# The second expert layer computed over sorted tokens in two parts

## The chip, the cores and the metric

The kernel runs on one core of a Trainium2 chip. The metric is the device time in microseconds (us) of one execution; lower is better. TensorE (PE) multiplies, VectorE (DVE), ScalarE (ACT) and GpSimd (POOL) do the rest, and SyncE (SP) issues the plain DMAs. TensorE's clock has two levels, 1.2 and 2.4 GHz; the profile shows the granted clock as a share of 2.4.

## The reference, cut to what matters

The input x holds 8 batches of 256 tokens of 128 channels, 2048 tokens, that is 16 token tiles of 128. Eight layers are added to it in turn: cross attention (att0), a mixing layer (ffn0), attention (att1), experts (moe1), attention (att2), experts (moe2), attention (att3), experts (moe3). The change rewrites moe2, whose reference is:

```python
def _L2_ffn_ref(x, ln_g, ln_b, rW, rb, W1, b1, W2, b2):
    z = _layernorm(x, ln_g, ln_b)              # E = 8 experts, TOP_K = 2
    probs = jax.nn.softmax(jnp.einsum('bth,he->bte', z, rW) + rb, axis=-1)
    topv, topi = jax.lax.top_k(probs, TOP_K)
    mask = jnp.sum(jax.nn.one_hot(topi, E, dtype=probs.dtype) * topv[..., None], axis=-2)
    w = mask / jnp.maximum(jnp.sum(mask, axis=-1, keepdims=True), 1e-08)
    hid = jax.nn.gelu(jnp.einsum('bth,ehf->btef', z, W1) + b1, approximate=False)
    outs = jnp.einsum('btef,efh->bteh', hid, W2) + b2
    return x + jnp.sum(outs * w[..., None], axis=2)
x = x + _L2_ffn_ref(_layernorm(x, axis=-1), ...)
```

Each token's result needs two of the eight experts only. W1 is 128x256 and W2 256x128 for each expert, all in float32.

## The kernel before, in words

The program is written out by hand, engine by engine, with semaphores. Each engine goes through the stages in the same order, and within a stage through numbered steps; where work of the next stage is put among the steps of this one, tables say so.

**Attention stages (att0, att1, att2).** They are pipelines over batches. A step of att2 has 8 beats u, one for each head; batch b is projected in one step, its row maxima are taken in the next, its columns, exponentials and averages follow, and it is finished and added to x (`residual`, L865) in the fourth. `steps_of` (L461) numbers the steps by `tail`, so that tail 0 is the first step in which no new batch starts, and (tail, u) names a place. The row maxima are DVE's (L912), eight in a step; PE may run at most two heads ahead of them. After the last batch there are four tail steps, 0 to 3.

**moe1, sorted.** The tokens are sorted by expert in two parts of 8 token tiles. For each part the router's logits are taken, a chain of small DVE operations picks two experts for a token (`route_pick`, L1101), `mark_picks` (L1139) marks them, PE ranks them (`rank_tokens`, L2241), and `place_tokens` (L1150) works out a row in a list of 23 tiles of 128 rows for each pick, each tile having one expert, and each tile's expert. POOL then scatters each token tile twice to DRAM by an indirect DMA (`send_row`, L1508 to L1523), 16 of them in a part; each waits for the third before it (IN_FLIGHT = 3). SP loads the lists' tiles back, two at a time, up to six ahead (`load_tile`, L660), when all sends of the part have landed. 46 tiles then go through a software pipeline (`sorted_tiles` on each engine; on PE L2265 to L2302). In its iteration j PE transposes tile j+2 (L2275), multiplies tile j+1 by the up and gate weights (L2280, 512 columns), transposes the hidden tile j (L2288) and multiplies tile j-1 by the down weights (L2295). ACT copies the transposed tile (L1810), takes the activation (L1815) and copies the transposed hidden tile (L1819); DVE multiplies the gate (L1247) and copies the output (L1254); SP stores it (L690). POOL fetches each token's two rows by indirect DMAs (`fetch_output`, L1525 to L1541), and DVE adds them to x by their weights (`join_outputs`, L1189). For the second part all routing pieces stand in iterations -2 to 3 (SORT_BEATS), its sends among tiles 4 to 17, and the joins of the first half in iterations 30 to 42; the second half is joined within att2's batches.

**moe2, dense.** All 8 experts are computed for all tokens, in 4 blocks of 512 tokens (`block_of` on PE, ACT and DVE; the middle two blocks are a hardware loop). For each expert and block PE does two up products of 512 columns (L2312), ACT a Gelu with bias on each (L1831), PE eight down products of 128 columns (L2224), and DVE four weighted additions to x (`add_y`, L1294). Its first 12 token tiles are normalised in tail steps 1 and 2 of att2: moments (L822, L829), the power -1/2 on POOL (`make_rstd_all`, L1389), the normalised tiles z (L837), transposed in tail step 2 (L1890). The last 4 follow after the last batch. Routing and the terms for bias and residual stand beside the first block (`beside_first_block`), and the first 12 tiles of att3 are normalised beside the last.

**att3** has one head. Its ten steps (`single_head`, from L2151 on PE) need att3's normalised tiles, 2 for each step, and x itself only for the addition at the end of a batch, two steps later: POOL adds the bias to x (`add_bias`, L1413), DVE adds the projection (L1060).

The names in the tables of the change: stats, rstd, norm, turn and turned are normalisation and transposing; logits, top, exp, first, second, mark, rank, place, weigh and load are the routing pieces in their order. Lines are those of the kernel before.

## Time and profile before

| | us |
|---|---|
| median of 3 runs | 861.91 (858.91 to 865.30) |
| the profiled execution's own time | 864.2 |
| its span, first to last instruction | 862.3 |
| PE busy in the span | 717.4 (83%) |
| DVE busy | 483.3 (56%) |
| ACT busy | 394.5 (46%) |
| POOL busy | 238.6 (28%) |
| mean granted TensorE clock | 0.938 |

The profiled execution took 2.3 us more than the median. In the rows below times are from the start of the span. In a timeline row the first number is the start, the second the time from the first start to the last end of the instructions merged in it, then engine, line, operation, output<-input, partitions x elements and type, the count, and in brackets the idle time before it with what ended it. The profile counts a float32 product as two matmul instructions and a float32 transpose as one.

### The profile page before, as it was taken

What the parts mean: (1) busy time and instruction counts of PE and PEld (TensorE: products, weight loads), DVE (VectorE), ACT (ScalarE), POOL (GpSimd) and SP (SyncE); (2) the same over time, 40 slices, a digit from 0 to 9 for tenths busy, and PEclk for the clock granted to TensorE, in tenths of its full rate; (3) what the DMA queues carried; (4) which work ended last, traced back from release to release, by engine and by line L of the source; (5) the groups of instructions that cost most, each with busy time, mean ns of one, the idle gap of its engine ahead of it and who ended that gap; (6) DMA issues with size and microseconds to landing.
All of it is one profiled execution on the core that took longest, in us unless ns stands there. A gap on an engine that the chain in (4) does not pass through costs nothing. (4 is left out here: it accounts for less than half of the span.)

```text
span 862.3 us, 14733 instructions
## 1 busy us (share of the span) xinstructions
PE 717.4 (83%) x4784; PEld 486.7 (56%) x4784; DVE 483.3 (56%) x1392; ACT 394.5 (46%) x837; POOL 238.6 (28%) x382
## 2 busy tenths in 40 slices
PE   1487788899998777998868786899999786679998
PEld 1255565556665445565534554667777675446665
DVE  4458756776777633435566865673335334444443
ACT  2356464466765454454425555453343454222221
POOL 3344454333331261516366543100001002000000
PEclk9999999999999895999958999799999999689999
DMA  9623323332222001333272320000000200033331
GB/s 272 168 57 99 93 52 92 89 94 69 64 58 58 11 34 32 102 90 107 81 205 67 82 75 2 1 1 1 1 0 1 83 1 0 3 88 97 98 97 63
DMA packets 76320, 57.96 MB, mean 67 GB/s; under 512 B 7400, under 2 KB 70120, under 8 KB 75768
## 3 DMA queue, kind: packets, MB, share of 16 engines
q1 hardware_dynamic: 74200, 52.85, 22.3%
q0 software_dynamic: 2048, 4.20, 1.6%
q8 instruction: 39, 0.64, 0.3%
q14 instruction: 33, 0.27, 0.1%
HBM read 25.37 MB, written 9.24 MB: 40 GB/s over the span
## 5 line engine op out<-in xcount | busy, mean ns | idle before, releaser
L912 DVE TENSOR_REDUCE negmax<-ps 128x2 f32<-128x512 f32 x256 | 169.5, 685 | 107.0 <-PE ps L1965 106.0
L1658 ACT ACTIVATE exps<-ps 128x512 f32<-128x512 f32 x256 | 148.3, 598 | 101.0 <-PE ps L1977 96.5
L1965 PE MATMUL ps<-stack 96*128 96x256 bf16 x512 | 103.6, 297 | 36.5 <-DVE negmax L912 20.0
L1977 PE MATMUL ps<-stack 99*128 99x256 bf16 x512 | 99.8, 285 | 18.5 <-DMA stack<-maxt 14.0
L1965 PEld LDWEIGHTS ps<-stack 96*128 96x128 bf16 x512 | 47.9, 103 | 62.0 <-DVE negmax L912 35.6
L1977 PEld LDWEIGHTS ps<-stack 99*128 99x128 bf16 x512 | 43.6, 100 | 60.1 <-DMA stack<-maxt 22.7
L1993 PE MATMUL ps<-exps,values 128*32 128x256 f32 x1024 | 73.3, 403 | 1.4 <-ACT exps L1658 1.4
L2224 PEld LDWEIGHTS ps<-pack_moe,ht 128*128 128x128 f32 x512 | 62.7, 194 | 16.4 <-issue 14.6
L1294 DVE SCALAR_TENSOR_TENSOR x_sb<-ps,weights,x_sb 128x128 f32<-128x128 f32 (+1 forms) x128 | 36.0, 344 | 61.8 <-PE ps L2224 61.6
L1831 ACT ACTIVATE ht<-ps,pack_moe 128x512 f32<-128x512 f32 x64 | 43.3, 686 | 57.6 <-PE ps L2312 56.0
L2224 PE MATMUL ps<-pack_moe,ht 128*128 128x128 f32 x512 | 63.0, 277 | 0.5 <-ACT ht L1831 0.5
L2312 PE MATMUL ps<-zt,pack_moe 128*128 128x512 f32 (+1 forms) x128 | 62.5, 611 | 0.0
L1844 ACT ACTIVATE gated<-ps 128x512 f32<-128x512 f32 x36 | 21.5, 597 | 76.4 <-PE ps L2341 76.4
L2280 PE MATMUL ps<-pack_moe,gated 128*128 x92 | 50.3, 630 | 0.0
L2352 PEld LDWEIGHTS ps<-pack_moe,ht 128*128 128x128 f32 x288 | 37.6, 193 | 19.8 <-issue 13.5
L1381 POOL TENSOR_SCALAR var_eps<-moments 128x12 f32<-128x12 f32 (+4 forms) x9 | 1.8, 201 | 166.3 <-DVE moments L829 136.1
L1284 DVE TENSOR_TENSOR ht<-ps,gated 128x512 f32<-128x512 f32 x36 | 24.9, 691 | 39.1 <-ACT gated L1844 39.0
L1523 POOL DMA_INDIRECT gathered<-z,placed x32 | 31.3, 980 | 52.6 <-DVE placed L1177 30.8
L1993 PEld LDWEIGHTS ps<-exps,values 128*32 128x32 f32 x1024 | 29.9, 113 | 21.3 <-issue 7.4
L2352 PE MATMUL ps<-pack_moe,ht 128*128 128x128 f32 x288 | 38.6, 277 | 2.7 <-DVE ht L1284 2.7
L1541 POOL DMA_INDIRECT late<-outputs_moe,placed x32 | 31.5, 986 | 31.1 <-DMA outputs_moe<-y_kept 15.7
L1468 POOL TENSOR_TENSOR qk_rest<-qk,qk_parts 128x512 f32<-128x512 f32 x24 | 27.8, 1157 | 44.3 <-DVE qk_parts L923 44.2
(221 smaller groups left out, 1317.0 us busy)
## 6 DMA issues: line engine op xcount, KB each, us to landing
stack<-qk_parts SPq DMA_DIRECT2D x168, 128.0 KB
stack<-weights_t SPq DMA_DIRECT2D x32, 256.0 KB, 3.2
pack_moe<-in_moe SPq DMA_DIRECT2D x1, 3076.0 KB, 16.4
outputs_moe<-y_kept SPq DMA_DIRECT2D x46, 64.0 KB
ht<-gathered SPq DMA_DIRECT2D x22, 128.0 KB
gathered<-y_kept SPq DMA_DIRECT2D x10, 256.0 KB, 3.6
pack_moe<-in_moe SPq DMA_DIRECT2D x1, 2129.0 KB
pack_moe<-in_moe SPq DMA_DIRECT2D x1, 1732.0 KB, 6.9
```

The source lines that it names most:

```text
L912: dve.tensor_reduce(negmax_of[b % 2][:, :, h:h + 1].rearrange("p t h -> p (t h)"), ps[:, h % 2, :].rearrange("p (t k) -> p t k", t=2), AX, ...
L1294: last = dve.scalar_tensor_tensor(out=xt, in0=ps[:, 4 + e % 2, t * D:(t + 1) * D], scalar=w, in1=xt, op0=ALU.mult, op1=ALU.add)
L1541: pool.indirect_dma_start(back[:, n, :], None, averaged[s, g], at).then_inc(back_in[n], 16)
L1658: nc.scalar.activation(exps[:, i, :], ps[:, 2 + h % 2, :], ACT.Exp, scale=scale)\
L1831: nc.scalar.activation(ht[:, e % 2, c, :], ps[:, 2 * (e % 2) + c, :], ACT.Gelu, bias=par(s, "b1")[:, k:k + 1]).then_inc(sem["h_ready"], 1)
L1965: last = pe.matmul(ps[:, h % 2, t * T:(t + 1) * T], st[0:MAXROW, h, 0, t * P:(t + 1) * P], st[0:MAXROW, h, 1, :], start=True, stop=True)
L1977: last = pe.matmul(ps[:, 2 + h % 2, t * T:(t + 1) * T], st[0:MAXROW + 3, h, 1, t * P:(t + 1) * P], st[0:MAXROW + 3, h, 0, :], start=True, ...
L1993: last = pe.matmul(ps[STRIP * k:STRIP * (k + 1), AV, r * T:(r + 1) * T], values[nh][:, buf(s, a), kt, u, :], exps[:, slot(s, a, u), kt * T ...
L2224: last = pe.matmul(ps[:, 4 + e % 2, t * D:(t + 1) * D], ht[:, e % 2, c, t * P:(t + 1) * P], par(s, "w2")[:, k * P:(k + 1) * P], start=(c = ...
L2280: pe.matmul(ps[:, (j + 1) % 2, :], taken_t[:, (j + 1) % 2, :], par(s, "experts")[:, bass.ds(at, 2 * T)], start=True, stop=True).then_inc(s ...
L2312: pe.matmul(ps[:, 2 * (e % 2) + c, :], par(s, "w1")[:, k * P:(k + 1) * P], zt[:, bass.ds(2 * blk, 2), 1:1 + T], start=True, stop=True).the ...
L2352: last = pe.matmul(ps[:, 4 + blk % 2, t * D:(t + 1) * D], ht[:, q % 2, 0, t * P:(t + 1) * P], par(s, "w2")[:, w * P:(w + 1) * P], start=(q ...
```

## The change

moe2 becomes sorted like moe1, with these differences. The up product has 256 columns in place of 512, there is no gate, and a bias is added within PSUM by a product of 3 rows of ones with 3 bfloat16 rows of biases (b1 and b2, each split in three parts). ACT's work for a tile is one copy with scale and bias and one Gelu; the copy of the transposed hidden tile is DVE's. The lists, tiles and weights are of the same size and number: 46 tiles, 23 in each part.

For the first part (token tiles 0 to 7) the normalisation and all routing pieces are put into att2's steps from tail -2 to tail 2, and its 16 sends at one per beat from tail 1, beat 1. Tiles 8 to 13 are normalised in tail 2 and 3, tiles 14 and 15 after the last batch. The second part's routing pieces are put one by one into iterations -1 to 8 of the tiles, its sends after tiles 9 to 22. The kept part of x (x plus its normalised value) is worked out by one DVE operation on a token tile in each of the iterations 5 to 20. The outputs of token tiles 0 to 7 are fetched and joined in iterations 25 to 43; those of tiles 8 to 15 at the start of att3: 16 fetches on POOL with the first additions of biases among them, and joins at the ends of DVE's steps 0 to 3. att3's normalisation goes in four groups of 4 token tiles: the first at tiles 36 to 41, the second right after the tiles, the third and the fourth in steps 1 to 5. The biases are split on POOL at the start of moe1 and spread by three small DMAs at the start of att2. The dense code of moe2 goes. moe1 and moe3 compute as before.

```diff
-    "moe2": [("router", 8), ("rb", 8), ("xg", 1), ("xb", 1), ("w1", 2048), ("b1", 16), ("w2", 2048), ("b2", 128)],
+    "moe2": [("router", 8), ("rb", 8), ("xg", 1), ("xb", 1), ("experts", 4096)],
...
-SORTED = ("moe1",)
-EXPERT = {"moe1": 768}
+SORTED = ("moe1", "moe2")
+EXPERT = {"moe1": 768, "moe2": 512}
...
+NORMED = {"moe1": (range(0, 8), range(8, 14), range(14, NT)), "moe2": (range(0, 6), range(6, 8), range(8, 14), range(14, NT))}
...
+    "moe2": {"stats": ((-2, 5), (-1, 5), (2, 5)), "rstd": ((-2, 7), (-1, 7), (2, 5)), "norm": ((-1, 0), (0, 0), (3, 5)),
+             "turn": ((-1, 2), (-1, 4), (0, 1), (3, 5), (3, 6)), "turned": ((-1, 3), (-1, 5), (0, 2), (3, 6), (3, 7)),
+             "logits": (0, 2), "top": (0, 3), "exp": (0, 4), "first": (0, 5), "second": (0, 6), "mark": (0, 7), "rank": (1, 0),
+             "place": (1, 1), "weigh": (1, 3), "load": (2, 3), "logits2": (3, 7)}}
+SEND_FROM = {"moe1": 14, "moe2": 9}
+SEND_EVERY = {"moe1": 2, "moe2": 1}
...
+              "moe2": {"logits": -1, "top": 0, "exp": 0, "first": 2, "second": 4, "mark": 5, "rank": 5, "weigh": 6,
+                       "place": 7, "load": 8}}
...
+JOIN_TILES = {"moe1": (30, 32, 33, 34, 36, 38, 40, 42), "moe2": (29, 31, 33, 35, 37, 39, 41, 43)}
+PLUS_TILES = range(5, 5 + NT)
+JOIN_STEPS = {0: (8,), 1: (9, 10, 11), 2: (12,), 3: (13, 14, 15)}
+LAST_TILES = {"stats": 36, "norm": 39, "turn": 40}
...
+SEND_TILE = {"moe1": 4, "moe2": 9}
...
+GROUPS = {"moe1": PART, "moe2": PART, "att3": tuple(range(t, t + BT) for t in range(0, NT, BT)),
...
-            sp.wait_ge(sem["x_updated"], done("x_updated", "moe2", 99))
+            pass_tiles("moe2")
+            wait(sp, "y_psum", "moe2", 0)
...
+                        sp.wait_ge(bias_split, 5)
+                        for k in range(3):
+                            sp.dma_start(bias_rows[k:k + 1, :], split[:, k, :]).then_inc(bias_in, 16)
...
+            def keep_of_norm(s):
+                r1 = rstd[:, 1, :]
+                dve.tensor_scalar(keep[:, 0, :], r1, 1.0, None, ALU.add).then_inc(sem["x_plus"], 1)
+                dve.scalar_tensor_tensor(out=keep[:, 1, :], in0=moments[:, :, 0], scalar=-1.0, in1=r1, op0=ALU.mult, op1=ALU.mult)\
+                    .then_inc(sem["x_plus"], 1)
+                wait(dve, "x_plus", s, 0, 1)
+            def plus_norm(s, t):
+                dve.tensor_scalar(x_sb[:, t, :], x_sb[:, t, :], keep[:, 0, t:t + 1], keep[:, 1, t:t + 1], ALU.mult, ALU.add)\
+                    .then_inc(sem["x_plus"], 1)
...
+                    if step in (2, 4):
+                        apply_all(s, step // 2 + 1, GROUPS[s][step // 2 + 1])
...
+                    if step in JOIN_STEPS:
+                        for t in JOIN_STEPS[step]:
+                            join_outputs("moe2", t)
+                    if step in (1, 3):
+                        stats_all(s, step // 2 + 2, GROUPS[s][step // 2 + 2])
...
+                if s == "moe2" and j == PLUS_TILES[0]:
+                    keep_of_norm(s)
+                if s == "moe2" and j in PLUS_TILES:
+                    plus_norm(s, PLUS_TILES.index(j))
+                if j in JOIN_TILES[s]:
+                    join_outputs(s, JOIN_TILES[s].index(j))
+                if s == "moe2":
+                    if j == LAST_TILES["stats"]:
+                        dve.wait_ge(loaded["att3"], 16)
+                        stats_all("att3", 0, GROUPS["att3"][0])
+                    if j == LAST_TILES["norm"]:
+                        apply_all("att3", 0, GROUPS["att3"][0])
...
+                    if s == "moe2" and 0 <= j < ALL_TILES:
+                        dve.wait_ge(sem["ht_psum"], done("ht_psum", s, 0, j))
+                        dve.wait_ge(sem["y_psum"], done("y_psum", s, 0, j - 2)) if j >= 2 else None
+                        dve.tensor_copy(turned[:, j % 2, :], ps[:, 3, 0:T]).then_inc(sem["ht_ready"], 1)
...
-            def add_y(s, blk, e):
-                wait(dve, "y_psum", s, blk, e)
-                wait(dve, "x_updated", s, blk, e - 1)
-                for t in range(BT):
-                    xt = x_sb[:, bass.ds(blk * BT + t, 1), :].rearrange("p a d -> p (a d)")
-                    w = weights[:, bass.ds(blk * BT + t, 1), e:e + 1].rearrange("p a d -> p (a d)")
-                    last = dve.scalar_tensor_tensor(out=xt, in0=ps[:, 4 + e % 2, t * D:(t + 1) * D],
-                                                    scalar=w, in1=xt, op0=ALU.mult, op1=ALU.add)
-                last.then_inc(sem["x_updated"], 1)
...
-                    wait(pool, "taken_psum", s, 0, SEND_TILE + n * 9 // 10)
+                    wait(pool, "taken_psum", s, 0, SEND_TILE[s] + n * 9 // 10)
...
+                    if s == "moe2" and t == 6:
+                        pool.wait_ge(loaded["att3"], 16)
+                        make_rstd_all("att3", 0, GROUPS["att3"][0])
...
+                    for t in range(2 * FETCHED_EARLY, NT):
+                        for k in range(2):
+                            fetch_output("moe2", t, k)
+                        if t == 11:
+                            add_bias(s, 0)
+                        if t == 13:
+                            make_rstd_all(s, 2, GROUPS[s][2])
+                            add_bias(s, 1)
+                    add_bias(s, 2)
+                    make_rstd_all(s, 3, GROUPS[s][3])
...
+            def gelu_tiles(s):
+                for j in range(-2, ALL_TILES):
+                    if 0 <= j + 2 < ALL_TILES:
+                        act.wait_ge(sem["taken_psum"], done("taken_psum", s, 0, j + 2))
+                        act.wait_ge(sem["up_psum"], done("up_psum", s, 0, j)) if j >= 0 else None
+                        nc.scalar.activation(taken_t[:, j % 2, :], ps[:, 2, 0:P], ACT.Identity, bias=par(s, "xb"),
+                                             scale=par(s, "xg")).then_inc(sem["taken_ready"], 1)
+                    if 0 <= j + 1 < ALL_TILES:
+                        i = (j + 1) % 2
+                        act.wait_ge(sem["up_psum"], done("up_psum", s, 0, j + 1))
+                        act.wait_ge(sem["ht_psum"], done("ht_psum", s, 0, j - 1)) if j >= 1 else None
+                        nc.scalar.activation(hidden[:, i, :], ps[:, i, 0:T], ACT.Gelu).then_inc(sem["h_ready"], 1)
+                    if j == SORT_BEATS[s]["exp"]:
+                        route_exp(s, 1)
+                    if j == LAST_TILES["turn"] + 1:
+                        copy_all("att3", [0])
...
+                        w = up_width(s)
+                        last = pe.matmul(ps[:, (j + 1) % 2, 0:w], taken_t[:, (j + 1) % 2, :],
+                                         par(s, "experts")[:, bass.ds(at, w)], start=True, stop=(s == "moe1"))
+                        if s == "moe2":
+                            last = pe.matmul(ps[:, (j + 1) % 2, 0:w], ones16[0:3, :], bias_rows[:, bass.ds(at, w)],
+                                             start=False, stop=True)
...
+                                             par(s, "experts")[:, bass.ds(at + (up_width(s) + c * D), D)], start=(c == 0),
+                                             stop=(c == 1 and s == "moe1"))
+                        if s == "moe2":
+                            last = pe.matmul(ps[:, 4, 0:D], ones16[0:3, :], bias_rows[:, bass.ds(at + up_width(s), D)],
+                                             start=False, stop=True)
...
-                        pe.matmul(ps[:, 2 * (e % 2) + c, :], par(s, "w1")[:, k * P:(k + 1) * P],
-                                  zt[:, bass.ds(2 * blk, 2), 1:1 + T], start=True, stop=True).then_inc(sem["up_psum"], 1)
...
```

## Rows read from the trace of the kernel before

**Rows 1.** Windows, moe2's bulk: stretch, length, busy PE/PEld/DVE/ACT/POOL, clock, DMA share, GB/s.

```profile
576.00:676.00 100.00, 100.00 (x592) 74.06 (x592) 38.48 (x147) 39.52 (x58) 2.48 (x2) 1.00 0.00 1
```

**Rows 2.** Timeline of PE: moe2's first product, and att3's first instruction.

```profile
546.75 1.88 PE L2312 MATMUL ps<-zt,pack_moe 128*128 128x512 f32 x4
...
676.39 0.60 PE L2156 MATMUL ps<-pack_consts,ctx_sb 128*96 128x128 f32 x4
```

**Rows 3.** Timeline of all engines in moe1: PE's work for one tile.

```profile
376.49 0.27 PE L2275 MATMUL ps<-pack_consts,ht 128*128 128x128 f32 x1
...
376.60 1.02 PE L2280 MATMUL ps<-pack_moe,gated 128*128 x2
...
377.46 0.38 PE L2288 MATMUL ps<-pack_consts,ht 128*128 128x128 f32 x2
...
377.68 0.61 PE L2295 MATMUL ps<-pack_moe,ht 128*128 x4
...
378.13 0.27 PE L2275 MATMUL ps<-pack_consts,ht 128*128 128x128 f32 x1
```

**Rows 4.** The same timeline: DVE's work for one tile.

```profile
378.08 0.42 DVE L1247 TENSOR_TENSOR ht<-ps,gated 128x256 f32<-128x256 f32 x1 [1.01 <-ACT gated L1815]
...
378.42 0.28 DVE L1254 COPY y_kept<-ps 128x128 f32<-128x128 f32 x1
```

**Rows 5.** Timeline of POOL: sends of part one and two, powers for 12 tiles.

```profile
324.17 0.96 POOL L1523 DMA_INDIRECT gathered<-z,placed  x1 [0.31 <-issue]
...
366.93 0.96 POOL L1523 DMA_INDIRECT gathered<-z,placed  x1 [0.30 <-issue]
...
728.69 2.28 POOL L1389 TENSOR_TENSOR rstd<-var_eps,neghalf 128x12 f32<-128x12 f32 x1
```

**Rows 6.** Timeline of DVE in att2's tail: after the last maximum, then the normalised tiles.

```profile
523.32 0.24 DVE L858 RECIPROCAL rden<-ps 128x16 f32<-128x16 f32 x1
...
537.41 3.16 DVE L837 TENSOR_SCALAR z<-x_sb,moments,rstd 128x128 f32<-128x128 f32 x12 [4.32 <-POOL rstd L1389]
```

**Rows 7.** Timeline of DVE in moe1: routing pieces, eight operations from the first to the second.

```profile
336.73 0.22 DVE L1109 TENSOR_REDUCE rs<-lg 128x8 f32<-128x64 f32 x1 [0.59 <-ACT lg L1723]
...
338.50 0.23 DVE L1118 SCALAR_TENSOR_TENSOR rt<-rt,lg 128x64 f32<-128x64 f32 x1
```

**Rows 8.** Timeline of SP's queue: the first loads of moe1's tiles.

```profile
326.41 6.94 SPq L672 DMA_DIRECT2D ht<-gathered  x4
```

**Rows 9.** Timeline of PE in moe1: first transposed tile, tile 3's hidden, tile 45's.

```profile
331.53 0.42 PE L2275 MATMUL ps<-pack_consts,ht 128*128 128x128 f32 x1
...
346.27 0.52 PE L2288 MATMUL ps<-pack_consts,ht 128*128 128x128 f32 x2
...
424.27 0.44 PE L2288 MATMUL ps<-pack_consts,ht 128*128 128x128 f32 x2 [0.27 <-DVE ht L1247]
```

**Rows 10.** Windows of moe1's start and its bulk (columns as in rows 1).

```profile
331.50:346.50 15.00, 11.01 (x38) 5.99 (x37) 8.08 (x36) 7.58 (x15) 0.00 (x0) 0.61 0.05 14
346.50:427.00 80.50, 74.98 (x405) 49.64 (x404) 38.23 (x127) 41.59 (x132) 35.93 (x39) 1.00 0.33 94
```

**Rows 11.** Timeline of ACT in moe1: an activation table is loaded.

```profile
335.14 1.28 ACT L1723 ACT_TABLE_LOAD   x1
```

**Rows 12.** Waits in moe1's bulk: engine, line, what it waited for: us, times, longest.

```profile
ACT gated L1810 <- remote: 2.0, 1, 2.0
```

**Rows 13.** The outputs' tensor of moe1: from a fetch's or store's issue to landing.

```profile
DMA to landing us min/median/max: 2.5/2.5/3.1
```

**Rows 14.** Timeline of PE in att3: the projections of two steps in turn.

```profile
701.14 0.70 PE L2165 MATMUL ps<-zt,pack_att 128*128 128x256 f32 x2
...
707.33 0.60 PE L2165 MATMUL ps<-zt,pack_att 128*128 128x256 f32 x2
```

**Rows 15.** Timeline of DVE in att3: the maxima of batch 1, the addition of batch 2.

```profile
688.14 0.69 DVE L1028 TENSOR_REDUCE negmax<-ps 128x2 f32<-128x512 f32 x1 [1.14 <-PE ps L2200]
...
707.53 0.42 DVE L1060 TENSOR_TENSOR x_sb<-ps,xb 128x256 f32<-128x256 f32 x1 [1.91 <-PE ps L1954]
```

More of the change, by code:

```diff
@@ L1410, in add_bias @@
                 wait(pool, "x_updated", s, d - 1)
-                wait(pool, "joined", "moe1", 0, 2 * d + 1) if s == "att2" else None
+                wait(pool, "joined", before(s), 0, 2 * d + 1) if before(s) in SORTED else None
                 bo = par(s, "bo").unsqueeze(1).to_broadcast([P, 2, D])
@@ L1823, in sorted_tiles @@
                         beside_last_tiles(EARLY_TILES.index(j))
-            def block_of(s, blk, first=False, final=False):
-                for e in range(E):
-                    for c in range(2):
-                        k = 2 * e + c
-                        wait(act, "up_psum", s, blk, k)
-                        wait(act, "y_psum", s, blk, e - 2)
-                        nc.scalar.activation(ht[:, e % 2, c, :], ps[:, 2 * (e % 2) + c, :], ACT.Gelu,
-                                             bias=par(s, "b1")[:, k:k + 1]).then_inc(sem["h_ready"], 1)
-                    if first:
-                        beside_first_block(s, e)
-                    if final and s == "moe2" and 5 <= e < 8:
-                        copy_all("att3", range(e - 5, e - 4))
@@ new lines, in experts @@
+            def experts(s):
+                for blk in range(NBLK):
+                    for i in range(E + 1):
+                        wait(act, "up_psum", s, blk, i)
+                        wait(act, "h_ready", s, blk, i - 2) if i >= 2 else wait(act, "h_ready", s, blk - 1)
+                        nc.scalar.activation(gated[:, i % 2, :], ps[:, 2 * (i % 2), :], ACT.Silu)\
+                            .then_inc(sem["gate_done"], 1)
+                        if blk == 0 and i < E:
+                            beside_first_block(s, i)
```

538 lines of the change are left out of this document (225 added, 313 removed), and 1 row of the table PACKS.

## The prediction

> **What bounds the kernel now.** I read the table of 40 slices first, where moe2 is the stretch in which PE is never below 9 tenths. The windows say it sharply: in 100 us of moe2 PE is busy 100.00 us at full clock, DVE 38 and ACT 40 [rows 1]. So PE alone bounds moe2, from its first product at 546.75 to att3's first instruction at 676.39, 129.6 us [rows 2]. Next I read the timeline of moe1, the sorted stage that moe2 is to copy. There the parts of a tile join without a gap: a tile takes 378.13 - 376.49 = 1.64 us, of which the product of 512 columns takes 377.46 - 376.60 = 0.86, two hidden transposes 377.68 - 377.46 = 0.22, two down products 378.13 - 377.68 = 0.45 and the transposed tile 0.11 [rows 3]. DVE needs 0.42 + 0.28 = 0.70 for it [rows 4]. A stage like this has a start, a bulk bound by PE, and a boundary between its parts, and I price moe2 so.
>
> **The change part by part.** It removes the 129.6 us. What comes in their place, from the same point of time on:
>
> *The start, moved later: +14.8.* Before, moe2's products needed only normalised tiles. Now the first tile waits for routing, placing and 16 sends. DVE's last maximum ends about 523.3 [rows 6]. Put among att2's steps before that are the eight tiles' normalisation (3.16/12 = 0.26 for each, 2.1, and as much again for their moments [rows 6]) and the pieces top to mark, some 20 operations at (338.50 - 336.73)/7 = 0.25, 5 us [rows 7]. Some 3 us of these fill gaps, so I count 6: the picks are marked at about 529.5. Ranking by PE and placing (8 operations, 2 us) follow: first send at 533. If the gaps hide all of it, it is 527, if nothing, 536. POOL's queue then holds 16 sends at 0.96 + 0.30 = 1.26, 20.2 us [rows 5]; between them two additions of biases (1.3) and the powers for tiles 8 to 13, as many as the 12 of the row at 2.28, with the two operations before 2.7 [rows 5]. That ends at 557.2, plus 1 for a pause, 558.2; the powers for tiles 14 and 15 stand behind it, 1.4, their tiles 0.7, and the sends' landing with the loads comes to about the same: in moe1 the load was issued 326.41 - 324.17 = 2.2 us after the last send began [rows 5, 8], and I give it 2 more. First transposed tile at 561.5, that is 14.8 after 546.75. Bounds 553 and 566, so +6 to +19. What goes with the old order helps here, and is in these numbers: DVE no longer waits 4.32 us for the powers of 12 tiles before att2's additions [rows 6].
>
> *From the first transposed tile to tile 3's hidden transposes: +10.5.* moe1 took 346.27 - 331.53 = 14.7, at a mean clock of 0.61 [rows 9, 10], since all pieces stood there. moe2 has three table switches between Gelu and the exponential, 3 x 1.28 = 3.8 [rows 11], and two and a half rounds at the lower level of 1.2 GHz, twice 1.4, so 7. Bounds 8 and 15.
>
> *The bulk, 42 tiles: +58.8.* PE's tile is 0.11 + 0.86/2 + 0.22 + 0.45 = 1.21 [rows 3]. The bias products run on 3 rows of bfloat16. No row has that shape; if they cost nothing the tile is 1.21, if as much as the float32 products of 256 and 128 columns, 0.43 + 0.22 more, 1.86. I take a quarter of that, since a float32 product counts as two instructions and each takes longer than a bfloat16 one of the same width: 0.16, and 0.03 for weights that can't load under so short a product; 1.40. DVE's copies (0.70) and the kept part (0.26) lie under it, ACT's copy and Gelu too. The bulk is 42 x 1.40 = 58.8; with the ends, 51 to 78.
>
> *Routing of the second part, tiles 4 to 8: +6.* In these five rounds DVE has 0.70 for the tile and nearly 0.3 for the kept part, with about 32 small operations (second, mark, weigh, place, load) at 0.25 [rows 4, 7]: 5 x 0.96 + 8.1 = 12.9 us against 5 x 1.40 = 7.0 of PE. The rest shows, since DVE goes in order and PE waits for its copy. 3 to 9. Their cover, if any, is the slack between rounds; the piece first, in tile 2, lies under a slow round.
>
> *The boundary at tile 23: +3.5.* The last send waits for the transposing of tile 22. Then: its start to the load's issue 2.2 [rows 5, 8], the load 2.1, releases 0.6; less one round. SP is behind this wait with the stores from tile 17 on, and DVE's copies wait for stores four tiles back; but the stores go out 0.4 us after the load, and land 2.5 later [rows 13], before the copy of tile 21. 0 if POOL is late by nothing and the landing is short, 6 if the sends lag.
>
> *Pauses: +6.5.* moe1's 42 tiles took 424.27 - 346.27 = 78.0 [rows 9] where 42 x 1.64 makes 68.9, and the early pieces of att2 on PE are some 2 of the 9.1. The rest are waits of 1 to 2 us on an engine for which the profile names no releaser but "remote", for instance 2.0 on ACT [rows 12]. moe1's code is written out tile by tile; the dense loop has none of them (100.00 of 100 us [rows 1]). I carry 6.5 over. The Trainium skill, page "Runtime: NRT & Kernel Launch", section on instruction fetch mechanics, says that fetching is hidden in straight code and that taken branches stall, which would favour unrolled tiles over the loop. By that rule this term is 0 and the result 6.5 us lower; the rows on both stages point the other way.
>
> *Joins and att3's tiles, tiles 29 to 45: +2.* Eight joins of two operations fit beside 1.40; the moments in tile 36 and the four normalised tiles in 39 (4 x 0.26) exceed it by some 1.5, the transposes on PE add 0.5. 1 to 4. *Drain: +1.7*, from tile 45's hidden transposes to att3.
>
> Sum: 14.8 + 10.5 + 58.8 + 6 + 3.5 + 6.5 + 2 + 1.7 = 103.8 for 129.6: 25.8 saved.
>
> *att3: +7.* POOL's 16 fetches can begin only when the last output is stored, 2.8 us after att3's first instruction (2.5 landing [rows 13]). At 1.26 each, with additions of biases and powers between, the eighth has landed at 14.7, the twelfth is issued at 18, the last has landed near 28.6. DVE joins tiles 9 to 11 before step 2's maxima: 14.7 + 0.7 + 1.3 of moments, 17 us after the start, where now the maxima of batch 1 come at 688.14 - 676.39 = 11.8 [rows 15]: 5 late. Tiles 13 to 15 hold step 3 in the same way until 30.5; after that the addition of batch 2 comes at 34 against 707.53 - 676.39 = 31.1 [rows 15], 3 late, and the maxima 3 to 5. I add 3 for the landing beside moe3's load, the third transposes and more time at the lower clock. Steps are 707.33 - 701.14 = 6.2 us apart [rows 14], a chain over all engines, so nothing later takes it back. Bounds 3 and 13.
>
> *At nothing:* the split of biases on POOL lies in POOL's wait for moe1's second placing; the three bias DMAs on SP stand at att2's start after the first stacks; moe1 and moe3 keep their work.
>
> Saved 25.8 - 7 = 18.8. Against the profiled execution that is 864.2 - 18.8 = 845.4. The median lies 2.3 below the profiled one, so for it 861.9 - 18.8 = 843.
>
> **The rivals.** A, *the start and att3 hide well*: sends from 527 and landing at once, first tile at 554 (-7.5), att3 only 3 late (-4), bias products at 0.08 (-4): 16 better, 827. For it: POOL is idle in att2's tail and DVE's gap before 537 is 4.3 us [rows 6]. Against: 16 sends have a fixed pitch.
>
> B, *VectorE bounds the round*: copy, copy, kept part, joins and routing in one order, with a releasing delay on each, make the round 1.64 as in moe1, 42 x 0.24 = 10 more, and the late fetches cost att3 10 in place of 7: 856. For it: DVE takes over a copy from ACT. Against: 0.96 of 1.40.
>
> C, the other side: *TensorE's clock stays low.* Waits in the routing rounds and in each tile bring the clock down to 1.2 GHz, and it stays there; each tile then takes 1.40 more. It decides at 18.8/1.4 = 13 tiles; over 30 tiles it is 42, so 885. For it: moe1 began at 0.61 with such gaps. Against: it then ran 80.5 us at 1.00 though PE was idle in 5.5 of them [rows 10]. The Trainium skill, page "TensorE: Matmul & The Clock Gate", section "A second HAM failure mode: psum-queue depth-cycling", tells of a kernel whose clock oscillated from short pauses between groups of matmuls; that speaks for C, and this trace disagrees with it so far.
>
> D, *the sends bound part two*: 16 sends and landings lag, and the boundary becomes 12 us: 852.
>
> **How the numbers follow.** Forecast 0.58, A 0.15, B 0.12, D 0.08, C 0.07. The forecast's own range, from its bounds, is 833 to 854. A and B widen it; with part of C left out I give 826 to 860. A measurement of this kernel tells 1% (8.6 us) from no change. Faster by over 1%, below 853.3: the forecast nearly whole, A, D for the most part: 0.82. Within 1%: most of B, the forecast's edge: 0.11. Slower by over 1%: C: 0.07.
>
> **What would show it.** In PE's timeline: the first transposed tile of moe2 at 561, a round of 1.40 in tiles 10 to 20, one gap near 3.5 us at tile 23, clock 1.00 in the bulk, rounds of 2 to 3 us in tiles 4 to 8 with PE waiting for DVE, att3's first instruction near 650, and DVE waiting for fetches in att3's steps 1 and 3. A round above 1.6, a low clock after tile 10, or a first tile after 566 would make it wrong.

## The result, and the profile after

The changed kernel takes 925.4 us (median of four runs, 911.9 to 935.3), before 863.0 (four runs, 858.9 to 865.3): ratio 1.061, 95% interval 1.051 to 1.071. Forecast were 843 us. The ratio is that of the two faster executions of the changed kernel (911.9 and 918.7, mean clock 0.865 and 0.853; the slower two are 932.1 at 0.833 and 935.3 at 0.830), and the profiled one, with a span of 933.5, is the slowest of the four, so the figures of the trace below are the upper end of the four.

Cut at the same events in both traces: moe1's first transposed tile, moe2's first work (its first transposed tile after the change, its first product before), att3's first context transposes, and the powers for moe3's twelve tiles. Columns are us between them:

| | moe1 begins | to moe2 | moe2 | att3 | rest | span |
|---|---|---|---|---|---|---|
| before | 331.5 | 215.2 | 129.6 | 52.3 | 133.6 | 862.3 |
| after | 327.5 | 243.1 | 157.7 | 68.2 | 137.1 | 933.5 |
| difference | -4.1 | +27.9 | +28.1 | +15.9 | +3.5 | +71.2 |

All three stages that I had priced came out longer. For moe2 the windows of the kernel after (columns as in [rows 1]) answer to [rows 1]:

```profile
580.00:600.00 20.00, 20.00 (x77) 12.70 (x76) 11.24 (x48) 5.05 (x13) 0.78 (x1) 0.50 0.15 41
600.00:620.00 20.00, 20.00 (x69) 12.43 (x67) 7.49 (x25) 5.41 (x13) 7.00 (x8) 0.50 0.21 66
640.00:660.00 20.00, 17.63 (x61) 11.24 (x61) 3.95 (x12) 4.59 (x11) 3.10 (x4) 0.50 0.19 54
700.00:720.00 20.00, 20.00 (x70) 12.99 (x69) 7.16 (x22) 5.72 (x13) 2.03 (x2) 0.50 0.12 34
```

PE is busy all the time, as forecast, but for 2.37 us at the boundary of the parts (in the third line), and the granted clock is 0.50, that is 1.2 of 2.4 GHz, through the whole stage. From 575 to 725 us PE stands still nowhere else, so no work on DVE, ACT or POOL shows any more: at this clock PE hides it all. Its timeline for one tile answers to [rows 3]:

```profile
596.26 0.47 PE L2280 MATMUL ps<-pack_consts,ht 128*128 128x128 f32 x1
596.53 1.06 PE L2286 MATMUL ps<-pack_moe,gated 128*128 x2
597.52 0.39 PE L2289 MATMUL ps<-values,ones 3*128 x1
597.84 0.69 PE L2298 MATMUL ps<-pack_consts,ht 128*128 128x128 f32 x2
598.32 1.06 PE L2305 MATMUL ps<-pack_moe,ht 128*128 x4
599.32 0.28 PE L2309 MATMUL ps<-values,ones 3*128 x1
599.53 0.47 PE L2280 MATMUL ps<-pack_consts,ht 128*128 128x128 f32 x1
```

A tile takes 599.53 - 596.26 = 3.27 us where 1.40 was forecast. The new shape in it is "3*128": the bias products, whose fixed operand has 3 rows. 42 x 3.27 = 137 is nearly the stage.

Ahead of the stage, att2's tail: DVE's last reciprocal, ACT's last copy of averages, and POOL's first and last send of part one, from the timelines of three engines:

```profile
560.23 0.26 DVE L903 RECIPROCAL rden<-ps 128x16 f32<-128x16 f32 x1 [6.49 <-PE ps L2042]
...
558.64 0.38 ACT L1701 ACTIVATE nd<-ps 128x256 f32<-128x256 f32 x1 [8.44 <-remote]
...
540.75 1.10 POOL L1535 DMA_INDIRECT gathered<-z,placed  x1 [4.93 <-PE ps L2002]
...
564.31 0.96 POOL L1535 DMA_INDIRECT gathered<-z,placed  x1 [0.31 <-issue]
```

Counted from moe1's first tile, the last reciprocal is at 232.8 (before: 544.5 - 331.5 = 213.0), so att2 itself became some 20 us longer; the sends begin at 540.75 where I had 533.

### The profile page after: what moved, and what is told of

Read it like the earlier page. It is cut to its first block and busy times, and to the rows that moved or that the text cites. A ratio compares the mean times of both kernels' runs of the same rounds, so it can differ in the third digit from the quotient of the medians.

```text
span 933.5 us, 15053 instructions
## 1 busy us (share of the span) xinstructions
PE 767.9 (82%) x4620; PEld 506.2 (54%) x4620; DVE 493.9 (53%) x1416; ACT 386.3 (41%) x861; POOL 305.3 (33%) x461
## 5 line engine op out<-in xcount | busy, mean ns | idle before, releaser
L1535 POOL DMA_INDIRECT gathered<-z,placed x64 | 62.6, 978 | 117.7 <-DVE placed L1225 60.5
L2286 PE MATMUL ps<-pack_moe,gated 128*128 x184 | 99.6, 635 | 0.0
L1553 POOL DMA_INDIRECT late<-outputs_moe,placed x64 | 62.3, 973 | 80.0 <-DMA outputs_moe<-y_kept 32.0
L2305 PE MATMUL ps<-pack_moe,ht 128*128 x368 | 78.5, 353 | 2.1 <-DVE y_kept L1318 2.0
L1306 DVE COPY ht<-ps 128x256 f32<-128x256 f32 x46 | 19.5, 425 | 69.0 <-PE ps L2298 61.7
L2298 PE MATMUL ps<-pack_consts,ht 128*128 128x128 f32 x184 | 49.9, 365 | 4.6 <-DVE ht L1311 2.5
L1875 ACT ACTIVATE gated<-ps,pack_moe 128x128 f32<-128x128 f32 x46 | 21.0, 457 | 74.1 <-PE ps L2280 70.6
L2298 PEld LDWEIGHTS ps<-pack_consts,ht 128*128 128x128 f32 x184 | 25.9, 173 | 41.7 <-issue 32.5
L1318 DVE COPY y_kept<-ps 128x128 f32<-128x128 f32 x92 | 26.5, 288 | 36.9 <-PE ps L2309 29.2
L2286 PEld LDWEIGHTS ps<-pack_moe,gated 128*128 128x128 f32 x184 | 42.1, 280 | 0.4
```

What stands on the lines that cost most here:

```text
L1535: pool.indirect_dma_start(gathered[g], at, z[:, t, :], None).then_inc(sent[i], 16)
L1553: pool.indirect_dma_start(back[:, n, :], None, averaged[s, g], at).then_inc(back_in[n], 16)
L2286: last = pe.matmul(ps[:, (j + 1) % 2, 0:w], taken_t[:, (j + 1) % 2, :], par(s, "experts")[:, bass.ds(at, w)], start=True, stop=(s == "moe1"))
L2298: last = pe.transpose(ps[:, 3, c * P:(c + 1) * P], hidden[:, j % 2, c * P:(c + 1) * P], ident)
L2305: last = pe.matmul(ps[:, 4, 0:D], turned[:, (j - 1) % 2, c * P:(c + 1) * P], par(s, "experts")[:, bass.ds(at + (up_width(s) + c * D), D)], ...
```

## The experiments

The question was why the clock stays low, then what is left when it doesn't. Kernels with "e2" in their expectation start from e2's code, not from the change; so do those that start from e5 or e7. Where a kernel ran once, its time stands without an interval.

**e1 and e2: take the bias products away, or make them full.** e1's edit:

```
-  start=True, stop=(s == "moe1"))
-  if s == "moe2":
-      last = pe.matmul(ps[:, (j + 1) % 2, 0:w], ones16[0:3, :], bias_rows[:, bass.ds(at, w)], ...)
+  start=True, stop=True)
```

and the same for the down product. e2's:

```
-  bias_rows = values[16]...bitcast(BF16)[0:3, 0:4 * E * P]
+  bias_rows = values[16]...bitcast(BF16)[:, 0:4 * E * P]
+  pool.memset(bias_rows[:, :], 0.0).then_inc(bias_zeroed, 1)      # in moe1, ahead of the three rows' DMAs
-  pe.matmul(..., ones16[0:3, :], bias_rows[:, ...])
+  pe.matmul(..., ones16[:, :], bias_rows[:, ...])
```

> Leaves out moe2's two biases (b1 and b2). Theory A, the bias products, whose fixed operand has 3 rows, are what keeps TensorE's clock at 0.50 in moe2: without them the granted clock is 1.00 there, a tile takes (3.27 - 0.53)/2 = 1.4 us, the stage some 80 us in place of 157.7, and the whole 850 to 862 us. Theory B, the clock is low because of what is left of a tile (a product of 256 columns, two of 128 and three float32 transposes): the clock stays 0.50, a tile takes 3.27 - 0.53 = 2.74 us, the stage some 134 us, the whole 908 to 915 us.

> The same two bias products with a fixed operand of 128 rows in place of 3: the bias rows 3 to 127 are zeros, so the sums are the same and no product is added or taken away. Theory A (the 3 rows are the reason): clock 1.00 in moe2, a tile 1.64 us, the stage 85 to 95 us, the whole 862 to 875 us. Theory B (the rest of the tile): clock 0.50, 3.27 us a tile, the whole within 1% of 925. If e1 is fast and this is slow, the bias products cost the clock for another reason than their rows, for instance by the time they take from the 128-row products.

Measured: e1 870.1 us, ratio to before 1.009 (1.007 to 1.012); e2 877.7, 1.018 (1.013 to 1.023). e2's windows, one of its tiles, and two starts of a tile from e1:

```profile
580.00:600.00 20.00, 15.61 (x112) 11.71 (x111) 14.72 (x62) 8.62 (x20) 5.00 (x5) 1.00 0.25 75
600.00:620.00 20.00, 15.19 (x106) 11.78 (x106) 10.30 (x33) 8.09 (x20) 10.53 (x11) 1.00 0.27 86
```

```profile
629.95 0.28 PE L2283 MATMUL ps<-pack_consts,ht 128*128 128x128 f32 x1
630.07 0.60 PE L2289 MATMUL ps<-pack_moe,gated 128*128 x2
630.51 0.27 PE L2292 MATMUL ps<-values,ones 128*128 x1
630.61 0.38 PE L2301 MATMUL ps<-pack_consts,ht 128*128 128x128 f32 x2
630.83 0.68 PE L2308 MATMUL ps<-pack_moe,ht 128*128 x4
631.34 0.22 PE L2312 MATMUL ps<-values,ones 128*128 x1
631.40 0.28 PE L2283 MATMUL ps<-pack_consts,ht 128*128 128x128 f32 x1
```

```profile
650.03 0.27 PE L2280 MATMUL ps<-pack_consts,ht 128*128 128x128 f32 x1
...
651.31 0.27 PE L2280 MATMUL ps<-pack_consts,ht 128*128 128x128 f32 x1
```

The products are the same in number and width, only their rows differ, and the kernel is 48 us faster by the medians (925.4 - 877.7), 38 us counted from the two faster executions (their mean 915.3); in the two profiled ones the stage is 99.1 in place of 157.7. The clock is 1.00 in these windows though PE stands still nearly a quarter of the time, and was 0.50 in the changed kernel in windows in which it never did. It isn't 1.00 throughout: e2's is 0.50 from 620 to 627 and from 644 to 647 us, each time after a pause of PE. That settles theory A against B, in kind; in size e1 is 8 us above A's upper end, with a stage of 96.6 us where 80 were expected, and e2 2.7 above, with 99.1 for 85 to 95. The undisturbed tile is 1.45 us, and 1.28 without any bias product (e1), so the two of full height cost 0.17. But with the clock restored the kernel is still slower than before.

**e3: the same thin products in moe1.** Two products of three zero rows (256 and 128 columns) join each tile of moe1.

```
+  if s == "moe1":
+      last = pe.matmul(ps[:, (j + 1) % 2, 0:2 * P], zero3[0:3, 0:P], zero3[0:3, :], start=False, stop=True, ...)
...
+  if s == "moe1":
+      last = pe.matmul(ps[:, 4, 0:D], zero3[0:3, 0:P], zero3[0:3, 0:D], start=False, stop=True)
```

> moe1's 46 tiles get the same two kinds of 3-row product as moe2's (256 and 128 columns, adding zeros); moe2 is untouched. Theory A in its strong form (such products pull the clock down wherever they are): moe1's clock falls from 0.99 to 0.50 and its tile from 1.64 to some 3.8 us, the whole over 1000 us. Theory B (moe2's smaller products are the reason): moe1 stays at 0.99 and its tile grows by at most 0.3 us where VectorE doesn't hide it, the whole 925 to 945 us.

Measured: 942.4 us (one run). Windows of moe1 and, in the last two lines, of moe2, then one tile of moe1 from PE's timeline:

```profile
330.00:346.00 16.00, 13.88 (x45) 6.67 (x45) 9.05 (x39) 6.82 (x14) 1.41 (x2) 0.50 0.05 15
346.00:427.00 81.00, 80.69 (x378) 43.27 (x378) 29.90 (x90) 34.73 (x103) 28.45 (x31) 0.98 0.27 80
...
605.00:610.00 5.00, 5.00 (x30) 3.10 (x28) 3.84 (x16) 2.14 (x5) 0.00 (x0) 1.00 0.19 54
620.00:625.00 5.00, 5.00 (x19) 3.38 (x18) 1.94 (x6) 0.99 (x3) 2.35 (x3) 0.50 0.28 92
```

```profile
379.76 0.33 PE L2285 MATMUL ps<-pack_consts,ht 128*128 128x128 f32 x1
379.93 1.02 PE L2291 MATMUL ps<-pack_moe,gated 128*128 x2
380.89 0.28 PE L2298 MATMUL ps<-values 3*128 3x256 bf16 x1
381.10 0.44 PE L2307 MATMUL ps<-pack_consts,ht 128*128 128x128 f32 x2
381.37 0.61 PE L2314 MATMUL ps<-pack_moe,ht 128*128 x4
381.92 0.23 PE L2321 MATMUL ps<-values 3*128 3x128 bf16 x1
382.07 0.33 PE L2285 MATMUL ps<-pack_consts,ht 128*128 128x128 f32 x1
```

The strong form of A falls: moe1 begins at 0.50 and still rises and stays, with its up product of 512 columns in place of 256. Thin products do harm in moe2's mix, not everywhere. Nor does the clock stay low in each execution of that mix: moe2's code is untouched in e3, and there the clock rose among the rounds with routing pieces and was 1.00 from 603 to 619 us, then 0.50 to 728, with no pause of PE over 0.72 us ahead of the fall; its moe2 took 142.9 us, e4's 138.8, the profiled changed kernel's 157.7. That is of the size by which the changed kernel's own four times differ, though only its slowest execution has a trace. The second finding I hadn't priced: moe1's tile is 2.31 us at full clock, 0.67 more than the 1.64 of [rows 3], where e2's two of full height cost 0.17, so that B's "at most 0.3" fails too.

**e4: enter the stage at full clock.**

```
+  if s == "moe2":
+      for _ in range(32):
+          pe.matmul(ps[:, 3, :], upper16[:, :], ones16[:, :].unsqueeze(1).to_broadcast([P, 4, P]), start=True, stop=True)
   turn_all(s, [len(CHUNKS[s]) - 1])
```

> 32 products of 128 rows and 512 columns that nobody reads, issued ahead of moe2's first tile: some 7 to 14 us more ahead of the stage. Theory C, the clock is low because the stage begins at 0.50 and what it does can't raise it, though it could hold it: the clock rises in the burst and stays 1.00, the whole 865 to 880 us. Theories A and B: the clock rises in the burst and falls back to 0.50 within the first tiles, the whole 930 to 945 us.

Measured: 922.8 us (one run). Windows, and the wait in the second of them from PE's timeline:

```profile
602.00:604.00 2.00, 2.00 (x12) 1.27 (x11) 0.65 (x2) 0.46 (x1) 1.60 (x2) 1.00 0.51 155
604.00:606.00 2.00, 0.77 (x5) 0.46 (x5) 0.89 (x4) 1.01 (x3) 0.20 (x1) 1.00 0.08 33
606.00:608.00 2.00, 2.00 (x9) 1.16 (x9) 0.96 (x3) 0.46 (x1) 0.88 (x2) 0.65 0.45 138
640.00:660.00 20.00, 20.00 (x69) 12.69 (x69) 4.30 (x12) 5.34 (x13) 4.57 (x5) 0.50 0.18 51
```

```profile
605.54 0.41 PE L2301 MATMUL ps<-pack_consts,ht 128*128 128x128 f32 x2 [1.23 <-DVE ht L1306]
```

C is right that the stage can hold the clock for a while: it is 1.00 from 580 to 606, with tiles of 1.88 us where nothing is waited for. It falls right after a wait of 1.23 us for DVE, and is then 0.50 to 705 us. The length of the wait alone doesn't decide: e9 below waits 1.24 us at 600 us and keeps 1.00. So my expectation "in the first tiles" was wrong in time and right in the end, and the whole is 7 us under its range.

**e7, e9, e10: how thin is thin.** The products of e2 with 32 and with 16 rows; and with 3 rows for the down product alone.

```
-  ones16[:, :], bias_rows[:, ...]
+  ones16[0:ROWS, :], bias_rows[0:ROWS, ...]     # ROWS = 32 in e7, 16 in e9; e10: 3 rows at the down product only
```

> e2's kernel with bias products of 32 rows in place of 128 (rows 3 to 31 zeros). If the clock goes by how many rows such a product has, 32 rows are nearer 3 than 128: clock 0.50 in most of moe2, 3.27 us a tile, the whole 915 to 930. If only the very thin product is harmful, clock 0.9 to 1.0 and the whole 870 to 885.

> e7's kernel (bias products of 32 rows, clock 0.83 to 1.00 in moe2, 880.4 us) with 16 rows. If the clock's answer is a smooth function of the rows, 16 lie where the clock changes between its two levels within moe2: 885 to 915 us. If anything above the thinnest product does, it is e7 again: 875 to 885. If 16 rows are as bad as 3, 0.50 in most of the stage and 915 to 930.

> e2's kernel with 3 rows in the down product's bias alone (128 columns), 128 rows in the up product's (256 columns). At 0.50 the 3-row time of a tile is then 0.21 us of 3.27 in place of 0.53. If it is the amount of thin work that counts, the clock is high for most of moe2 and the whole 875 to 890. If any thin product in each tile does it, clock 0.50 and 915 to 930.

Measured, one run each: 880.4, 905.7 and 878.8 us; moe2 took 105.7, 129.9 and 99.8. Windows around the boundary of the parts, e7 and then e9:

```profile
620.00:622.00 2.00, 0.00 (x0) 0.00 (x0) 0.00 (x0) 0.00 (x0) 0.00 (x0) 1.00 0.30 87
624.00:626.00 2.00, 2.00 (x9) 1.45 (x9) 0.42 (x1) 0.38 (x1) 0.00 (x0) 0.50 0.15 44
630.00:632.00 2.00, 2.00 (x13) 1.36 (x13) 0.72 (x2) 0.88 (x3) 0.00 (x0) 1.00 0.35 98
```

```profile
622.00:624.00 2.00, 0.00 (x0) 0.00 (x0) 0.00 (x0) 0.00 (x0) 0.00 (x0) 0.87 0.44 126
...
630.00:632.00 2.00, 2.00 (x8) 1.01 (x7) 0.41 (x2) 0.46 (x1) 0.00 (x0) 0.50 0.03 9
...
660.00:680.00 20.00, 20.00 (x69) 12.65 (x69) 7.53 (x28) 5.05 (x12) 6.33 (x8) 0.50 0.21 58
```

In both PE stands still for 3.5 to 3.7 us before part two's first load, and the clock falls to 0.50. With 32 rows it is back at 1.00 by 630; with 16 it stays at 0.50 to 691 us, 3 us before the last tile is transposed; e9's stage is part fast and part slow, for this reason and not because 16 rows make a middle clock. e10 shows that thinness alone isn't fatal: with 3 rows in the narrower product the clock falls three times in the stage and is back each time within a few us. What these runs bear out: the clock falls at pauses (in e3 without a long one), and whether the plain tiles that follow bring it back is what the rows decide. For the rounds with routing pieces this isn't shown: there it rose with 3 rows in e3, and not in the changed kernel.

e7's undisturbed tile is 1.88 us, as with 3 rows in e4, and e2's is 1.45: at full clock, 32 rows are as dear as 3, and both 0.43 dearer than 128. The Trainium skill, page "TensorE: Matmul & The Clock Gate", section "Why this matters for your kernels", says that one product of 32 rows takes the time of one of 128; between products of full height this case disagrees, by that 0.43 us for two.

**e5, e8, e11: att2's tail.** e5 moves the two early norms by beats, e8 issues the second 8 of part one's 16 sends behind the last powers, e11 puts all routing pieces into the last beat and all sends behind att2.

```
e5:  "norm": ((-1, 0), (0, 0), ...)  ->  ((-1, 2), (0, 1), ...);  "turn", "logits" ... "second" one or two beats later
e8:  0 <= n < 2 * len(GROUPS[nxt][0])  ->  0 <= n < len(GROUPS[nxt][0]); the rest in sorted_tiles after make_rstd_all
e11: "logits" ... "weigh": (3, 7); all 16 send_row in sorted_tiles after make_rstd_all
```

> e2's kernel (877.7 us) with part one's two early norms of moe2 asked of VectorE later (the first by two beats, the second by one), and what follows them with them, so that VectorE doesn't stand before GpSimd's reciprocal root (3.5 and 2.2 us in the trace after) with att2's maxima queued behind it. Theory P, these stands push att2's tail and the routing with it: the first send comes 2 to 5 us earlier, the stage starts 2 to 5 us earlier, the whole 873 to 876. Theory Q, the beats themselves set it: the pieces come a beat later, the first send is 1 us later or the same, the whole 877 to 880.

> e2's kernel with the second 8 of part one's 16 sends behind the last reciprocal root instead of in one train. Theory R, the train of indirect sends holds up ScalarE's stand of 8.4 to 9.2 us ahead of its last copy of averages in att2 (named remote, in four of the five traces with the change): with 8 sends in the train the stand ends some 10 us earlier and att2 is over 5 us sooner, while the stage starts at the same time or up to 6 us later, since the last sends are later. Theory S, the stand is ScalarE's own (code or something that doesn't depend on the sends): it stays at 8 to 9 us and the stage starts 6 to 12 us later.

> e2's kernel with part one's routing (logits, picks, ranks, places, weights) in att2's last beat in place of beats 2 to 11 of its last three batches, and all 16 sends behind att2. Nothing is left out. Theory U, the pieces among the maxima and the train of sends lengthen att2's tail: its last reciprocal of the denominators comes 8 to 14 us earlier than in e2 (561.8 us, with moe1 at 331.4), and the stage starts some 12 to 20 us later, since the 16 sends (20 us) then lie open. Theory V, the tail is long because of the two early norms and TensorE's lower clock there: the last reciprocal comes less than 4 us earlier, and the stage starts over 20 us later. The whole 888 to 900 by U, over 900 by V.

Measured: e5 874.8 us (ratio to before 1.016, 1.010 to 1.023), which lies in P's range but isn't to be told from e2; its first send comes 212.3 us after moe1's first tile against e2's 210.7, and its stage starts 1.7 later, so Q holds for what P was about, and DVE's stands were not the reason. e8 882.4 and e11 897.8 (one run each). ACT's last copy of averages in e8, and DVE's last reciprocal in e11:

```profile
555.33 0.38 ACT L1707 ACTIVATE nd<-ps 128x256 f32<-128x256 f32 x1 [3.47 <-PE ps L2024]
```

```profile
544.96 0.23 DVE L905 RECIPROCAL rden<-ps 128x16 f32<-128x16 f32 x1
```

e8: the stand named "remote" is gone (R). From moe1's first tile the copy comes at 223.0, in e2 at 560.2 - 331.4 = 228.8. It buys nothing, since the stage starts 4.8 us later, behind the later sends: part one's start waits for the sends, and ACT's stand lies under them. A stand of this size is missing in e4, e5 and e12 too, which have one of 3.6 to 4.3 us ahead of an exponential instead, and their copies come no earlier than e2's (231.0, 229.3 and 232.6). e11: the last reciprocal comes 215.0 us after moe1's first tile, in e2 230.4, before 213.0. So the pieces and sends among att2's maxima lengthen it by 15.4 us, more than U's 14; 2.0 over before are left, with the early norms still in their place. Some 7.4 of the 15.4 arise at ScalarE's last copy alone: it comes 10.4 us after the one before it in e2, where the stand is, 4.7 in e8 and 3.0 in e11. With pieces and sends behind, the stage starts 20.5 us later (261.4 against 240.9).

**e6: att3 without the second way back.**

```
+  if s == "moe2" and g: return                     # fetch_output
+  if s == "moe2" and t >= NT // 2: (two memsets); return    # join_outputs
```

> e2's kernel without the second part's way back: the 16 fetches of tiles 8 to 15 on GpSimd and their 16 adds on VectorE during att3 are left out (two tiny memsets a tile keep the counts). If they make att3's excess (68.7 us in e2 against 52.3 before), att3 falls to 52 to 56 us and the whole to 860 to 865. If the excess is something else (the clock, which is 0.66 to 0.83 there, or steps that wait for a group's norm), att3 stays above 62 and the whole above 870.

Measured: 864.1 us (one run), att3 60.5 us: between the two expectations. The fetches and adds cost 8.2 of the 16.4 us that e2's att3 (68.7) has over before. In e6's timeline of PE three steps are 8.3 to 8.4 us long, one of them the first below, and those between them 6.8 to 7.0:

```profile
692.12 0.60 PE L2194 MATMUL ps<-zt,pack_att 128*128 128x256 f32 x2
...
700.40 0.60 PE L2194 MATMUL ps<-zt,pack_att 128*128 128x256 f32 x2
...
707.21 0.60 PE L2194 MATMUL ps<-zt,pack_att 128*128 128x256 f32 x2
```

Before, steps are 6.2 apart [rows 14]. Three groups of normalised tiles are now turned and copied inside att3's steps; that can be most of the other 8.2, though no run took it away alone. The clock is a rival for it: 0.97 in the kernel before from 676 to 729 us, 0.85 in e2 from 671 to 740, and 0.91 in e6 from 670 to 730.

**e12: keep TensorE busy in its pauses.**

```
+  keep_busy(3, 12) if s == "att2" and d == B - 1 else None          # ahead of the last turn_averages
+  keep_busy(7, 16) if s == "moe2" and j + 2 == PART_AT[1] else None # products of 512 columns
```

> e5's kernel (874.8 us) with products that nobody reads where TensorE stands still: 12 of 512 columns in att2's last batch while it waits for ScalarE's last copy of averages (6.6 us in e2), 16 at the boundary of the two parts while it waits for the first load of the second (3.8 us). In e2, e7 and e9 the clock falls to 0.50 at that boundary. Theory W, the fall comes from the standing still: with the 16 the clock stays 1.00 across the boundary and the tiles after it take 1.7 us and not 2.5 to 2.8, worth 3 to 5 us; the 12 add 0 to 3 at the start of the stage: the whole 866 to 872. Rival X, the fall is hidden by other waits or the fillers outlast the waits: 874 to 879. In no case under before's 861 to 863.

Measured: 875.0 us, ratio to before 1.013 (1.006 to 1.020), the same as e5. Windows from the boundary on, with PE's filler ahead of the first load of part two:

```profile
620.00:622.00 2.00, 2.00 (x11) 0.94 (x10) 0.55 (x2) 0.00 (x0) 0.00 (x0) 1.00 0.08 33
624.00:626.00 2.00, 2.00 (x18) 1.71 (x17) 0.82 (x3) 1.16 (x4) 0.00 (x0) 1.00 0.34 97
```

```profile
619.35 3.62 PE L2040 MATMUL ps<-ones,upper 128*128 128x512 bf16 x16
623.18 0.33 PE L2289 MATMUL ps<-pack_consts,ht 128*128 128x128 f32 x1 [0.21 <-DMA ht<-gathered]
```

W holds at its place: with the filler the clock stays 1.00 across the boundary, where e2 has 0.50 until nearly 627, and the next two tiles take 1.64 and 1.46 us, in e5 2.35 and 2.25. X holds for the sum: moe2 is 97.5 against e5's 97.7, so what the tiles behind the boundary gain, 1.5 us, is lost again among the waits that follow; the clock falls at 637.7 in a wait of 2.48. The 12 fillers end some 3 us after the copy that they were to bridge. The stage starts 3.5 us later than e5's (246.1 against 242.6 from moe1's first tile), but that isn't their doing: att2's first copy of averages, long before them, is already 3.4 us later (128.3 against 124.9). No version that I ran beats the kernel before.

## Why the prediction was wrong

The forecast was 18.8 us saved, with 0.07 on a slower kernel. The profiled execution missed its 845.4 us by 89.9. The step that failed by most is the bulk's clock, taken as 1.00, with 0.07 for rival C: 52 us. Behind it come the tile's bias term, the start of the stage, and att3. The terms that each event closes, forecast, in the kernel after, and in e2, where the clock is restored (us, against before where signed):

| term | forecast | after | e2 |
|---|---|---|---|
| start of moe2, later by | 14.8 | 27.9 | 25.7 |
| first tile to tile 3's hidden | 10.5 | 13.9 | 10.5 |
| from there to tile 45's hidden | 76.8 | 139.2 | 85.6 |
| drain | 1.7 | 4.6 | 3.0 |
| att3 | +7 | +15.9 | +16.4 |

*The bulk, the bias term.* "I take a quarter of that ... 0.16, and 0.03 for weights" was the step that failed first in the sum. The tile without bias, 1.21, was near: e1 has 1.28. But two products of three rows cost 0.60 there even at full clock (1.88 in e4), and 0.67 in moe1 (e3), three times my 0.19 and about my upper bound of 0.65, which I had built from full-height rows and thought safe. The 0.03 in it, for weights that can't load under so short a product, rests on no row, and no run shows it by itself; full-height products, loads and all, cost 0.17. I reasoned about columns and number format and not about the rows of the fixed operand, which was the new thing in the edit.

*The clock.* Rival C named the low clock and a price, "1.40 more" a tile: it is 3.27 - 1.88 = 1.39. That the figures agree is luck, since C doubled a tile of 1.40 and the tile was 1.88, which the lower clock did not double. I gave C 0.07 because moe1 had kept 1.00 with idle time in it [rows 10]. The row was true and the inference wrong: moe1's products are all of full height, and its up product is twice as wide. Nor was its cause the one C gave, "waits in the routing rounds and in each tile": e2 has more waits than the kernel after, and its clock comes back after each fall. The thin products keep it from coming back in plain tiles; why it never rose in the changed kernel's first rounds, as it did in e3's, stays open. For the size of the two parts, e7 is the kernel after with the clock mostly up: moe2 105.7 us. So 157.7 - 105.7 = 52.0 of the profiled stage is clock (37.2 by the same code in e3's 142.9), and 105.7 - 99.1 = 6.6 the longer tile of the thin products where nothing else hides it.

*The start.* "Some 3 us of these fill gaps, so I count 6" was the second failing step: the first send was forecast at 533, 528.9 on the clock of the kernel after (its moe1 is 4.1 earlier), and came at 540.75, 11.8 late. From there to the first tile I had 28.5, it was 29.8; the term for sends, powers and landing stands. e11 shows what att2 as a whole pays: pieces and sends among the maxima lengthen it by 15.4. I had added DVE's busy time and nothing for the sends. e8 shows that the second half of the train alone, which stands beside the last copy, is worth 5.8; for the rest my reading, which no run takes apart, is that the maxima, ScalarE's exponentials and TensorE's rows go round in a chain in which each piece makes the others late. The clock was lower with it, 0.76 in 510 to 530 us against 0.91 before.

*Routing of part two, boundary, pauses.* Together 16 us beside the bulk's 58.8 and 2 for joins. In the kernel after, only the boundary can be seen (2.37 us of waiting against 3.5), since a slow PE covers the rest. In e2 the same stretch is 85.6 us, of which 42 x 1.45 = 60.9 is the undisturbed pace, so 24.7 for these terms against 18: 6.7 too few. What I had missed in them is that the pause at the boundary also costs tiles at the lower clock. The pauses were also worked out from a wrong reading: the row at 346.27 in [rows 9] is tile 2's hidden transposes, tile 3's are at 348.05. moe1's 42 tiles thus took 76.2 us, 7.3 over 68.9, in place of 9.1; with the 2 for att2's pieces the term is 5.3, not 6.5. (The 14.7 before it is 16.5; the +10.5 doesn't use it.)

*att3.* The reasoning on fetches and adds gave 3 to 5 of the +7, and e6 gives 8.2 for them. "I add 3 for the landing beside moe3's load, the third transposes and more time at the lower clock" stood for what is 8.2 too, with the groups turned inside att3's steps and the lower clock. Both halves were sized too small.

*At nothing* held: moe3 and the rest are 1.6 us longer in e2, and moe1's tiles take 90.4 us against 89.2.

Had each bias product been of full height, the forecast would still have been wrong in sign: e2 is 1.8% slower, by the start (10.9 over), the stretch from tile 3 (8.8 over) and att3 (9.4 over). Of the other rivals, B and D were a few us in size and A went the other way: none of them decided. The 0.07 on a slower kernel was all C's, so the forecast gave no chance to what e2 shows: start, pauses and att3 priced too low all at once.

## What to carry to other kernels

Read the rows of every new product's fixed operand before its columns: with a bias of three rows added by a product TensorE ran 150 us at 1.2 GHz in the profiled execution, and padding it with zero rows to the full 128, at no further instruction in the stage, gave back 38 to 48 us; with 32 rows the clock came back too, but the tile stayed 0.43 us longer. When small pieces are laid among the steps of a chain that already passes between four engines, don't price them by the busy time of one engine: some 10 us of VectorE's work and the sends beside it made 15 us of delay, of which 7 stood in one wait of ScalarE's. And before expecting gain from filling a pause, ask whether something else ends the stage: the filler held the clock across the boundary and the time didn't move. And where executions of one kernel differ by 2.5%, one trace shows one of them: compare the stage in a second run of the same code before calling its clock the kernel's.

## What the runs showed of the hardware

- A product of 3, 16 or 32 rows between products of 128 costs about 0.2 us more than one of 128 rows, at full clock (1.88 against 1.45 us for a tile with two; 1.63 for one, in e10). The full-height bias products are the cheaper ones: 0.17 us for two (1.45 against e1's 1.28).
- Within moe2 the granted clock fell to 0.50 in each pause of TensorE of 1.97 to 3.94 us that met it at 1.00, or within 3 us of its end (e1, e2, e5 to e12). Shorter ones went both ways: it fell after 1.23 us (e4) and 1.70 (e10), and not after 1.24 (e9), 1.59 (e2) and 1.80 (e6); in e3 it fell with no pause over 0.72.
- Between plain tiles it was back at 1.00 within five tiles with bias products of 32 or 128 rows; with 3 or 16 (after, e3, e4, e9) it stayed at 0.50, with TensorE busy 20.00 of 20.00 us, in e3, e4 and e9 up to the stage's last 9 to 10 us. In rounds with routing pieces it rose with 3 rows in e3 and with 16 in e9, and in moe1's wider mix with 3 rows it rose as usual.
- ScalarE stood 7.8 to 9.2 us ahead of one copy, with no releaser on the core, in the kernel after and in seven experiments (e1, e2, e3, e6, e7, e9, e10), and went on 0.7 to 1.0 us after the powers behind the twelfth send had begun. In e4, e5 and e12, whose train of sends has a break after the eighth (2.5 to 3.0 us from start to start in place of 1.26), it stood 3.6 to 4.3 us ahead of an exponential; in e8, with 8 sends there, and in e11, with none, it didn't stand. What it waits for no row names.
